# Two of four token gathers of an expert round wait for a later matmul of TensorE

## The reference

```python
xn = layernorm(x)
x = x + attention(xn) + moe(xn)          # layer 0, then a second layer of the same shape

# attention: 16 heads of 8, unit-length q and k, full softmax over the 1024 keys of the batch
# moe: 64 experts, top 3 of each token, capacity 64 slots per expert
buf[e, pos] = xf[tok]                     # tokens gathered into the slots of their experts
h = gelu(buf @ w1[e] + b1[e])             # 64 slots x 128 -> 512
y = h @ w2[e] + b2[e]                     # 512 -> 128
out[tok] += gate * y[e, pos]
```

## Time and profile before

| | |
|---|---|
| median of the runs | 533.34 us (533.27 to 535.56) |
| the profiled execution | 531.58 us |
| its span, from the first to the last instruction | 529.8 us |
| PE busy | 487.6 us, 92% |
| ACT busy | 371.2 us, 70% |
| DVE busy | 307.0 us, 58% |
| POOL busy | 146.1 us, 28% |
| mean granted clock of PE | 0.977 of full speed |
| first and last gather at L388 | 103.5 and 250.8 us |

### The profile page before, as it was taken

How to read it: one execution, slowest core, us unless ns; L and a number is a source line. 1 busy time by engine, 2 the same in 40 slices (tenths; PEclk the granted TensorE clock), 3 DMA queues, 4 the chain that set the end, 5 groups by cost and what they waited for, 6 DMA issues and landing times.

```text
span 529.8 us, 11354 instructions
## 1 busy us (share of the span) xinstructions
PE 487.6 (92%) x4602; PEld 260.5 (49%) x4602; DVE 307.0 (58%) x814; ACT 371.2 (70%) x459; POOL 146.1 (28%) x133
## 2 busy tenths in 40 slices
PE   2975999999999999999998999998899999999996
PEld 1654223343454554464454332332466767776775
DVE  6799997734343434432531107158756993995895
ACT  3735888876889789889788899979734635543641
POOL 4049300110232032032000254525470657300120
PEclk9986799999999999999998999999999999999999
DMA  5200000193478778878732611100100020000000
GB/s 147 80 2 0 2 1 1 32 315 108 113 236 294 234 247 277 243 234 285 208 109 93 194 31 31 33 14 11 37 16 0 17 50 16 21 1 2 21 0 21
DMA packets 38540, 50.01 MB, mean 94 GB/s; under 512 B 3580, under 2 KB 20248, under 8 KB 38488
## 3 DMA queue, kind: packets, MB, share of 16 engines
q1 hardware_dynamic: 35524, 43.84, 25.6%
q0 software_dynamic: 2560, 5.25, 5.4%
q10 hardware_dynamic: 404, 0.20, 0.1%
HBM read 45.07 MB, written 4.19 MB: 93 GB/s over the span
## 4 chain that ended last, share of the span: by engine, by line
PE 48%; ACT 17%; DVE 6%; issue 5%; DMA 1%; POOL 0%; POOLq 0%; DVEq 0%
ACT region_b L545 11%; PE bank L1307 10%; PE bank L1560 9%; PE scores L1551 9%; PE scores L1293 5%; PE bank L1353 3%; PE bank L1341 3%; ACT xn L551 2%; PE bank L1363 2%; PE bank L1423 2%; DVE region_a L1052 2%; ACT L545 2%; ACT L551 2%; DVE base L1063 1%; PE bank L1318 1%
## 5 line engine op out<-in xcount | busy, mean ns | idle before, releaser
L545 ACT ACTIVATE region_b<-scores 128x1024 f32<-128x1024 f32 x256 | 242.5, 1044 | 52.1 <-PE scores L1293 51.8
L1307 PE MATMUL bank<-region_b 128*16 128x256 f32 x2048 | 147.8, 388 | 0.2 <-DVE av_out L799 0.2
L1293 PE MATMUL scores<-region_b 32*128 32x512 f16 x512 | 84.0, 389 | 14.9 <-ACT region_b L545 13.8
L388 POOL DMA_INDIRECT region_a<-xn_rows,slot_token x32 | 32.5, 1015 | 161.6 <-DVE h_rows L893 108.5
L607 ACT ACTIVATE region_b<-scores,small_cols 128x512 f32<-128x512 f32 x64 | 43.6, 685 | 47.2 <-PE scores L1551 47.2
L1307 PEld LDWEIGHTS bank<-region_b 128*16 128x16 f32 x2048 | 41.6, 95 | 57.1 <-issue 41.7
L1560 PEld LDWEIGHTS bank<-region_a,region_b 128*128 128x128 f32 x512 | 62.0, 192 | 15.1 <-issue 15.0
L1293 PEld LDWEIGHTS scores<-region_b 32*128 32x128 f16 x512 | 21.0, 91 | 94.3 <-ACT region_b L545 69.2
L1560 PE MATMUL bank<-region_a,region_b 128*128 128x128 f32 x512 | 62.5, 275 | 0.0
L1551 PE MATMUL scores<-x_rows,region_a 128*128 128x512 f32 x128 | 60.8, 597 | 0.0
L1063 DVE SCALAR_TENSOR_TENSOR base<-bank,g,base 128x128 f32<-128x128 f32 x128 | 36.0, 343 | 26.2 <-PE bank L1560 25.8
(11 more groups left out here) (233 smaller groups left out, 560.0 us busy)
## 6 DMA issues: line engine op xcount, KB each, us to landing
region_a<-in_L_ffn_w SPq DMA_DIRECT2D x64, 512.0 KB, 5.4
region_a<-in_L_ffn_b SPq DMA_DIRECT2D x17, 128.0 KB, 7.4
slot_out<-slots_io SPq DMA_DIRECT2D x8, 256.0 KB, 8.4
region_a<-in_L_attn_x SPq DMA_DIRECT2D x4, 256.0 KB, 4.8
xn_rows<-xn SPq DMA_DIRECT2D x1, 1024.0 KB, 5.1
region_a<-in_L_ffn_W SPq DMA_DIRECT2D x1, 1024.0 KB, 6.0
out<-base SPq DMA_DIRECT2D x4, 256.0 KB, 2.3
region_a<-xn_rows,slot_token POOLq DMA_INDIRECT x32, 3.8
```

Source lines behind the costliest of these rows:

```text
L388: g.indirect_dma_start(ring_in[m % RING], None, xn_rows, bass.IndirectOffsetOnAxis(IDX[:, m:m + 1], 0), bounds_check=T - 1, oob_is_err=Tru ...
L545: a.activation(PR[:, n % PBUF, 2 * h:2 * h + 2, :], S[:, 2 * h:2 * h + 2, :], ACT.Exp, scale=SCALE).then_inc(s["exp_done"], 1)
L1293: last = mm(S[:, j], KT[head, hg, keys], QT[head, hg, BLK * c:BLK * c + BLK], start=True, stop=True)
L1307: last = mm(AV[32 * j:32 * j + VW, cols], VA[:, tile, HG * (g % NHG) + j, :], PR[:, st % PBUF, j, cols], start=(st == 0 and half == 0), st ...
```

## The change

One more wait stands on POOL, ahead of the third gather of every set of four but the first set. It asks for the values of the third tile of the round before the one that the set is for; PE runs these in that round's fourth tile (step 3). The first two gathers go as they did, and the fourth follows the third.

```diff
             for m in range(NPAIR):
                 if m >= RING and m % RING == 0:
                     pool.wait_ge(s["h_sb"], m)
+                if m >= RING and m % RING == 2:
+                    pool.wait_ge(s["av_done"], MOE_FROM + ROUND_TILES * (m // RING - 1) + 3)
                 g.indirect_dma_start(ring_in[m % RING], None, xn_rows, bass.IndirectOffsetOnAxis(IDX[:, m:m + 1], 0),
                                      bounds_check=T - 1, oob_is_err=True).then_inc(ring_in_x[m % RING], 16)
```

## The result

The changed kernel takes 572.83 us (median of 4 runs, 569.78 to 576.27) against 533.31 us for the kernel before beside it (4 runs, 532.44 to 535.56): a ratio of 1.0746, 95% interval 1.0696 to 1.0796. It is slower by 39.5 us. The prediction said slower by 29, 562 in a range of 535 to 570: the direction and the place hold, the size does not. In two later comparisons, with more runs of the kernel before, the unaltered change came out at 568.83 and 572.75, 34.8 and 38.6 us over it.

A forecast was written before the change was run, and what follows sets the result against it. The prediction took PE, running in order, to bound the rounds. On the profiled 531.58 us it added 19.2 of waits and 9.8 of clock, 560.6; with the runs' median 1.8 higher, 562, in a range of 535 to 570.

The forecast's parts named there:

- What bounds the kernel: Expert rounds: PE, in order, busy 19.45 of 19.80 us, so its waits lengthen the program by nearly their whole length.
- Where the gathers move: POOL's queue: gathers three and four start 2.76 us later, in set 1 only 0.37; nothing queued behind them matters.
- The slack: Gather four's start to PE's first gathered transpose: 4.2 us in sets 2, 3, 6, 7, and 3.8 in 4, 5.
- The landing of gather four: Behind the down-weight loads: gather four takes 7.2 us, so PE waits 3.0 us in four sets, 3.4 in two.
- q0 has no packets while q1 carries the down weights: Sign expected on the DMA queues: the gathers' queue stays empty during the weight loads, gather four landing near 7 us.
- The clock: PE after each long wait: the granted clock falls, costing 1.6 us in each of six sets, 9.8 in all.
- Rival (3): PE after the waits: full wait of 19.2 us but the clock stays, giving 552.5 us; chance 0.20.
- The sum: Whole program: 19.2 us of PE waits and 9.8 of clock, giving 560.6 on the profiled execution, 562 as median.
- The range: Whole program: 535 to 570 us, leaving out slipping through and faster, 0.20 together.
- Slipping through: Queue arbitration: gather four lands in 3.0 to 4.0 us despite the full load queue, giving 534 us; chance 0.17.
- part of the way: Gather four among the loads: lands in 4.6 to 6.3 us, giving 537 to 547, around 540; chance 0.22.

The follow-up runs named there:

- a1x: Changed kernel with SyncE's four down-projection loads held until gather four of the next set has landed, third run (ten runs): 533.86 us, ratio 0.9968.
- a4x: Changed kernel with the new wait ahead of gather four alone instead of gather three, third run (ten runs): 536.31 us, ratio 1.0067.
- a5: Changed kernel with thirty filler identity transposes on PE before its wait for the gathers of sets 2 to 7: 561.34 us, ratio 1.0504.
- b1x: Changed kernel with only the third and fourth down-projection loads held until gather four has landed, second run: 550.36 us, ratio 1.0193.
- a1: Changed kernel with the four down-projection loads held until gather four of the next set has landed, first run: 540.26 us, ratio 0.9839.
- a1r: Changed kernel with the four down-projection loads held until gather four of the next set has landed, second run: 541.71 us, ratio 0.9815.
- a2: Changed kernel without the down-projection loads of rounds 1 to 7, all rounds using those of round 0: 544.49 us, ratio 0.9801.
- d1: Changed kernel with the new wait before the first gather of a set, so all four go late: 595.94 us, ratio 1.0832.
- b1: Changed kernel with only the third and fourth down-projection loads held until gather four has landed, first run: 554.91 us, ratio 1.0082.

## Why the prediction was right and where it was wrong

**What bounds the kernel: right.** PE works in order and is the bound of the rounds; 24.5 to 25.4 us of waiting and the clock behind it are the whole growth of the rounds, and where the wait was taken away (a1x) they were 135.0 us again.

**Where the gathers move: right.** 2.78 us later against 2.76; the distance from the values' end over POOL's start to gather four as worked out; in set 1 a wait of 0.42 instead of 0.30, where 0.67 was predicted, the smallest term of all. Nothing behind them on POOL mattered: its wait for VectorE in seven sets is now 127.6 us, more than in the earlier trace rows.

**The slack: right.** 4.2 or 3.8 us were worked out; in after PE is ready at 163.80, 4.45 us after gather four's start. a1x, with landings up to 3.9, waits nowhere.

**The landing of gather four: the step that was mis-sized.** I took 7.2 us; it was 8.1 in the mean and 9.1 in set 2. 0.9 us too little in six sets are 5.4 us, and the waits grew by 24.5 us where the sum had 19.2. The 7.2 is the shorter landing of the earlier trace rows and that of the third load in the earlier trace rows, and the gather does land about with the third load. What I missed is that the earlier trace rows show the loads with no late gather among them. In before the third load lands 6.8 to 9.1 us after the four loads' start, 7.9 in the mean of sets 2 to 7. In after it is 8.9 to 10.6, 9.7 in the mean, with two gathers in the same stream; the fourth of round 1 went from 8.4 in the earlier trace rows to 10.8. The queues of after in round 1 show what happens (packets, MB, share of 16 engines; 160 to 160.5, then 161 to 162, then q0 alone from 161 to 164.2 and from 164.2 to 168.5 us):

```profile
q1 hardware_dynamic: 65, 0.13, 95.7%
...
q0 software_dynamic: 25, 0.07, 103.1%
q1 hardware_dynamic: 114, 0.20, 58.1%
...
q0 software_dynamic: 32, 0.07, 32.3%
...
q0 software_dynamic: 32, 0.07, 22.2%
```

And the same two gathers in a1x, 160.1 to 161.35 and 161.35 to 163.6 us:

```profile
q0 software_dynamic: 32, 0.07, 24.1%
...
q0 software_dynamic: 32, 0.07, 21.0%
```

"q0 has no packets while q1 carries the down weights" was half right. There are none with data from 158.1 to 161, while q1 moves 0.38 MB; from 161 on both queues move. What the prediction did not have is that the two late gathers go one after the other. A gather is 32 packets in these traces, 16 of 4 KB and 16 of 4 bytes. Gather three's first data packet starts 3.0 to 3.2 us after POOL's instruction in after, 1.7 in a1x. Gather four's starts 4.9, 5.0, 6.1, 4.3, 2.9 and 5.6 us after its instruction (sets 2 to 7), 1.7 to 2.0 in a1x. In all six sets that is within 0.8 us of gather three's landing. So the larger part of the delay stands ahead of the gather's first packet; the rest is that its 16 data packets start over 1.1 to 3.5 us instead of 0.6 to 1.0. The landing follows the end of the last data packet by 0.4 to 0.8 us, in a1x by 0.3 to 0.7: it is the data that are late, not the semaphore's increment by itself. In a4x, where gather three has landed 0.8 to 2.5 us before gather four's first packet, that packet starts after 2.5 to 3.2 us, about as gather three's does in after. This would explain why one gather among the loads costs so much less than two; it is read from the packets and was not tested by a kernel of its own.

How long a single packet takes can't be read from the shares: in the us from 161 to 162 the two queues' shares add up to 161% of the 16 engines, so the times of packets overlap. In bytes the us is like one of before: 0.27 MB for both queues, against 0.26 MB of q1 alone in before from 157 to 158. What the gathers move in it, the loads don't (q1 moves 0.20).

The Trainium skill, DMA: Bandwidth & Descriptors, section Queues, rings and completion order, says that each DMA engine takes turns between its queues a packet at a time. The trace agrees so far that both queues move data from 161 to 162; in what order the engines take their packets is not shown. What I had drawn from that rule as a rival, that a small gather slips through in 3 to 4 us, is contradicted: 7.6 to 9.1 us in six sets.

**The clock: right in kind, too small.** 1.6 us a wait, 9.8 in all, were predicted from the one fall in the earlier trace rows. It was 2.3 to 2.4 for each of the five waits inside the rounds, since in four of six sets PE worked some 6 us at half clock and not the 3 to 4 of the earlier trace rows. In all it came to 11 to 12. That the total is this close to 9.8 is in part luck: behind the sixth wait only 0.7 us are seen, and the fall of the earlier trace rows, which before has and after has not, is set off against it. Rival (3), the full wait with the clock staying, is what a5 makes artificially: 561.34 on a kernel that otherwise takes 568.83.

**The sum.** Predicted: 19.2 + 9.8 = 29.0. Found in the second comparison's trace: 25.4 + 12.1 = 37.5, with 0.2 before set 0, 37.7 of span. The missing 8.5 are 6.2 of waiting and 2.3 of clock.

**The range was cut where it should not have been.** The bounds in the earlier trace rows, 3.0 to 4.7 us a set, gave 571.7 at the upper end, and I took 570, since "not all six will be at the end". The 571.7 was itself too low by its own rule: with 0.4 us less slack in sets 4 and 5 it would have been 572.5. Waits of one pattern are not six independent draws: they ran from 3.41 to 5.01, each above the value taken for its set (3.0, or 3.4 in sets 4 and 5). And an upper bound from loads that had no gather among them was itself no bound. The three medians, 568.83, 572.75 and 572.83, lie on both sides of 570.

**The rivals.** Slipping through (534) and part of the way (537 to 547) are excluded for the change as it stands; near the two ends of the latter are a4x (536.3) and b1x (550.4). The cost has a steep place: by the rounds, a4x loses 4.4 us, b1x 13.9 and after 36.7.

**What stays open.** What holds the gathers is not shown. A strict order behind the loads is excluded by the sets in which the gather lands first; but whether the first packet waits for its descriptors, for a place in a queue or for its share of the engines can't be told, since the traces give when a packet starts and not what it waits for. A change of the packets' size or of the queue that carries the gathers was not tried. What decides whether the clock falls behind a wait of about 2 us is open as well. Nor is it known why the kernel before took 550 to 552 us in two comparisons; there is no trace of it from there. Of the kernels beside it, `a1` and `a1r` had rounds of 136.1 and 135.7 us, and the traces had up to 8 us more before set 0 and up to 10 us more behind set 7. Where before took its ordinary 534 us, no kernel here beats it by more than can be measured; beside a before of 550 us a1 was 1.6 to 1.9% under it, and that is not explained.

| fourth gather, sets 2 to 7 | what is ahead of it | landing | PE waits, all sets | ratio |
|---|---|---|---|---|
| a1x | nothing | 2.8 to 3.9 | 0 | 0.9968 |
| a2 | 512 KB out and shifts, in part | 3.7 to 5.5 | 3.2 | 0.9801 |
| a4x | nothing, loads 0.3 us behind (one gather moved) | 4.4 to 6.4 | 3.9 | 1.0067 |
| b1x | two loads | 4.7 to 6.6 | 10.0 | 1.0193 |
| after | four loads, issued 1 us before | 7.6 to 9.1 | 24.8 | 1.0746 |
| d1 | four loads and three gathers | 6.6 to 8.8, start 2.7 later | 41.4 | 1.0832 |

(The ratios of a2 and d1 are against a before of 550 and 552 us, and do not compare with the others.)

## What to carry to other kernels

When a small transfer is moved, ask which bulk transfer of another queue it now moves past: two gathers of 64 KB, 2.8 us later and well within their slack, cost 37 us because they changed sides with 2 MB of loads. If both must be issued close together, let the bulk wait for the small one's completion: a1x shows that this costs nothing where the bulk has time. Count the small transfers too: the second of two late ones started its data only when the first was nearly in. And size a landing under load by rows of the small transfer itself under that load, not by the load's own landing, and count the clock on top of the waits on PE, here 2.3 to 2.4 us for each wait of 3.4 to 5.0.

## What the runs showed of the hardware that was not expected

- The fourth gather of a set, 128 rows of 512 bytes, takes 2.8 to 3.9 us in a1x, with no down load around it, and 6.6 to 9.1 among 2 MB of loads, whether it starts 1.05 or 3.75 us after them (after, d1). The slowing is mutual: the fourth load of round 1 took 8.4 us in before and 10.8 in after, with two gathers among the loads.
- Of two late gathers the second's first data packet starts within 0.8 us of the first's landing in the six sets of after, 2.9 to 6.1 us after its own instruction; in a1x the distance is 1.7 to 2.0.
- Identity transposes with the same weights and the same moving tile, back to back, take 0.115 us each (3.44 us for 30), where the four of gathered tokens take 0.15 each and I had counted 0.28.
- After idle times of 3.4 to 5.0 us PE worked at half clock for 3.4 to 6.3 us. After 1.86 to 2.45 us in b1x the clock had a mean of 0.72 over the next 6 us, and after 1.85 and 1.98 us in b1; but after 2.27 us in b1, and after 2.07 us in a5, where 3.44 us of filler stood before it, it was 1.00.
